# Cross-attention scores: probabilities as half-precision bits copied as 32-bit words, one maximum over two banks, and the exponential's table loaded at the stage's start

## The reference

```python
def _L0_xattn_ref(x, cond, Wq, bq, Wkv, bkv, Wp, bp):
    q = (x @ Wq + bq).reshape(1, B * N, H, hd)
    kv = (cond @ Wkv + bkv).reshape(1, -1, 2, H, hd)
    k, v = (kv[:, :, 0], kv[:, :, 1])
    ...
    q = _fq_sym(q, axis=-1)        # whole numbers from -127 to 127, times a step
    k = _fq_sym(k, axis=-1)
    v = _fq_sym(v, axis=2)
    attn = jnp.einsum('bhqd,bhkd->bhqk', q, k)
    attn = jax.nn.softmax(attn.astype(jnp.float32), axis=-1)
    attn = _fq_unsigned(attn, axis=-1)   # whole numbers from 0 to 255, times a step
    out = jnp.einsum('bhqk,bhkd->bhqd', attn, v)
    out = jnp.transpose(out, (0, 2, 1, 3)).reshape(B, N, C)
    return out @ Wp + bp
```

## Time and profile before

| | us |
|---|---|
| three runs | 1235.86, 1240.04, 1241.66 |
| median | 1240.04 |
| profiled execution | 1237.78 |
| its span, first to last instruction | 1236.1 |
| of that the scores stage (about 399 to 872) | 473 |
| PE, DVE, ACT busy over the span | 1003.9, 852.8, 700.4 |

### The profile page before, as it was taken

One profiled execution on the slowest core, in us unless ns is written; L12 is line 12 of the kernel. 1 busy time (PEld: TensorE's weight loads), 2 busy tenths in 40 slices (PEclk: granted clock), 3 DMA queues, 4 the chain that ended last, 5 costly groups with the idle time before them and its releaser, 6 DMA issues. The chain is left out here.

```text
span 1236.1 us, 21867 instructions
## 1 busy us (share of the span) xinstructions
PE 1003.9 (81%) x8049; PEld 682.7 (55%) x8049; DVE 852.8 (69%) x1409; ACT 700.4 (57%) x1039; POOL 243.6 (20%) x216
## 2 busy tenths in 40 slices
PE   4888996999457777777777777777779989999998
PEld 3745744888345444444444444444557765556566
DVE  6857546999687899999999999999661521111126
ACT  3453362455426899999999999999223202212221
POOL 1134063556250200000000000000533610000014
PEclk9999998999678799999999999999779989999999
DMA  8200004110000000000000000000040395131215
GB/s 320 96 1 1 1 2 154 51 34 17 9 0 13 31 1 2 1 0 0 0 0 0 0 0 0 0 0 0 1 151 27 135 379 230 60 116 64 69 56 182
DMA packets 24854, 68.14 MB, mean 55 GB/s; under 512 B 2722, under 2 KB 6818, under 8 KB 23778
## 3 DMA queue, kind: packets, MB, share of 16 engines
q1 hardware_dynamic: 20114, 52.48, 11.3%
q0 software_dynamic: 4400, 14.42, 3.7%
q10 hardware_dynamic: 288, 0.52, 0.1%
HBM read 49.07 MB, written 18.35 MB: 55 GB/s over the span
## 5 line engine op out<-in xcount | busy, mean ns | idle before, releaser
L1313 DVE TENSOR_REDUCE cs_top<-cs_s_b 128x1 f32<-128x512 f32 x256 | 164.8, 685 | 16.7 <-PE cs_s_b L1342 7.6
L1350 PE MATMUL cs_tp<-ident,cs_p_int 128*128 128x128 f16 x2048 | 158.4, 221 | 7.5 <-ACT cs_pT L1293 2.8
L1287 ACT ACTIVATE cs_p_int<-cs_s_b,cs_bias,cs_step_now 128x1024 int16<-128x1024 f32 x128 | 154.1, 1204 | 11.6 <-DVE cs_bias L1320 5.3
L1301 DVE TENSOR_REDUCE cs_top<-cs_s_a 128x1 f32<-128x1024 f32 x128 | 155.5, 1215 | 7.2 <-PE cs_s_a L1342 7.2
L1350 PEld LDWEIGHTS cs_tp<-ident,cs_p_int 128*128 128x128 f16 x2048 | 122.1, 98 | 60.3 <-issue 45.6
L1342 PE MATMUL cs_s_b<-k_parts,q_int 96*128 96x512 bf16 x256 | 79.0, 391 | 93.4 <-ACT cs_p_int L1287 93.1
L1287 ACT ACTIVATE cs_p_int<-cs_s_a,cs_bias,cs_step_now 128x1024 int16<-128x1024 f32 x128 | 152.8, 1194 | 0.0
L1293 ACT CAST cs_pT<-cs_tp 128x1024 bf16<-128x1024 int16 x128 | 129.5, 1012 | 3.3 <-PE cs_tp L1350 2.7
L2159 PE MATMUL ff_h<-ff_experts,ff_zgT 128*128 x368 | 115.1, 467 | 1.0 <-ACT ff_zgT L1798 0.9
L1446 POOL TENSOR_TENSOR co_o<-co_o,v_step 128x512 f32<-128x512 f32 x8 | 10.7, 1331 | 467.6 <-DVE co_o L1468 467.6
L1342 PE MATMUL cs_s_a<-k_parts,q_int 96*128 96x512 bf16 x256 | 79.4, 393 | 22.9 <-ACT cs_p_int L1287 18.7
(11 more groups left out here) (278 smaller groups left out, 2099.0 us busy)
## 6 DMA issues: line engine op xcount, KB each, us to landing
ff_experts<-in_experts_dram SPq DMA_DIRECT2D x8, 2176.0 KB, 14.6
slots<-sa_zero SPq DMA_DIRECT2D x1, 5888.0 KB, 25.8
ff_zg<-slots POOLq DMA_DIRECT2D x23, 256.0 KB, 2.9
run_y<-ff_yv SPq DMA_DIRECT2D x23, 256.0 KB, 2.0
ff_raw<-in_weights_dram SPq DMA_DIRECT2D x6, 768.0 KB, 5.8
ck_raw<-in_ctxT_dram SPq DMA_DIRECT2D x8, 512.0 KB, 3.3
stage<-in_cwkv_dram SPq DMA_DIRECT2D x2, 1024.0 KB, 6.8
out_dram<-x_res SPq DMA_DIRECT2D x8, 256.0 KB, 2.0
```

Source lines behind the costliest of these rows:

```text
L1287: nc.scalar.activation(p_int[:, u, half * HALF:(half + 1) * HALF], s[:, :], ACT.Exp, bias=bias[:, u:u + 1], scale=step_now[:, h:h + 1], ac ...
L1301: nc.vector.tensor_reduce(top[:, u, 0:1], s_a[u][:, :], AX_X, ALU.max).then_inc(max_ok, 1)
L1313: nc.vector.tensor_reduce(top[:, u, 1 + c:2 + c], s_b[:, c * 512:(c + 1) * 512], AX_X, ALU.max).then_inc(max_ok, 1)
L1350: ins = nc.tensor.transpose(tp[:, k, :], p_int[:, u, key:key + P].bitcast(F16), ident16[:, :])
```

## The change

- The copies out of `tp` no longer convert. `pT` becomes a 16-bit integer tile that holds the same bits as `p_int`, and the product reads it as half-precision floats, in which a whole number p up to 255 is p times 2^-24. ACT moves two of them at once as a 32-bit integer (at most 255 * 65536 + 255, less than 2^24); DVE's copy stays one of 16-bit elements. `v_int` becomes half precision. The output is multiplied by `P_UNIT` = 2^24 where it was copied (L1332).
- The two maxima over the banks of `s_b` become one over both, and `sb_ok` counts once per unit, after the second matmul.
- ACT computes a one-column exponential at the stage's start, ahead of its first unit.

```diff
+P_UNIT = 2.0 ** 24
...
-        pT = sb("cs_pT", [P, 2, KT, P], BF16)
-        top = sb("cs_top", [P, 2, 3], F32)
+        pT = sb("cs_pT", [P, 2, KT, P], I16)
+        top = sb("cs_top", [P, 2, 2], F32)
...
+        table = sb("cs_table", [P, 1], F32)
...
-                nc.scalar.copy(pT[:, u, HKT:KT, :], tp[:, :, :].bitcast(I16)).then_inc(rb_ok, 1)
+                nc.scalar.copy(pT[:, u, HKT:KT, :].rearrange("p k q -> p (k q)").bitcast(I32),
+                               tp[:, :, :].rearrange("p k q -> p (k q)").bitcast(I32)).then_inc(rb_ok, 1)
+            nc.scalar.activation(table[:, :], ident16[:, 0:1], ACT.Exp)
             units(act, step)
...
-                    for c in range(2):
-                        v_.wait_ge(sb_ok, 2 * n + c + 1)
-                        nc.vector.tensor_reduce(top[:, u, 1 + c:2 + c], s_b[:, c * 512:(c + 1) * 512], AX_X,
-                                                ALU.max).then_inc(max_ok, 1)
-                    v_.wait_ge(max_ok, 3 * n + 3)
+                    v_.wait_ge(sb_ok, n + 1)
+                    nc.vector.tensor_reduce(top[:, u, 1:2], s_b[:, :], AX_X, ALU.max).then_inc(max_ok, 1)
+                    v_.wait_ge(max_ok, 2 * n + 2)
...
-                    nc.vector.tensor_copy(o_raw[:, t - 1, :], out[:, :]).then_inc(out_read, 1)
+                    nc.vector.tensor_scalar(o_raw[:, t - 1, :], out[:, :], P_UNIT, None, ALU.mult).then_inc(out_read, 1)
...
-            def scores(t, h, s, half, made, each_bank=False):
+            def scores(t, h, s, half, made):
...
-                    if each_bank or c == 1:
-                        ins.then_inc(made, 1)
+                ins.then_inc(made, 1)
...
-                    scores(t, h, s_b, 1, sb_ok, each_bank=True)
+                    scores(t, h, s_b, 1, sb_ok)
...
-                        ins = nc.tensor.matmul(out[:, head * D:(head + 1) * D], pT[:, u, k, :],
+                        ins = nc.tensor.matmul(out[:, head * D:(head + 1) * D], pT[:, u, k, :].bitcast(F16),
...
-        v_int = sb("v_int", [P, KT, C], BF16)
+        v_int = sb("v_int", [P, KT, C], F16)
```

## The result

| | before | after |
|---|---|---|
| median of the runs made beside each other, us | 1236.58 (six, 1233.26 to 1241.66) | 1247.96 (six, 1246.95 to 1251.32) |
| profiled execution, us | 1237.78 | 1248.07 |
| its span, us | 1236.1 | 1246.3 |

The ratio is 1.009, with a 95% interval of 1.0063 to 1.0116: the changed kernel is slower by 11.4 us. The forecast was 11.6 us more than before. Its 1251.6 stood on the first three runs of before (median 1240.04); with three more that median is 1236.58, and this is nearly all of the 3.6 us between 1251.6 and 1247.96.

The account below looks back on a forecast made before the run. A closed loop ACT, PE, DVE, ACT around the single buffer `s_b` was taken as the bound, 3.54 us a period. Terms +16.7 - 0.5 - 2.8 - 0.4 - 1.4 = +11.6 us on median 1240.04 gave 1251.6 us, range 1243 to 1260.

Parts of the forecast that it names:

- The maximum's wait and merge: Usual `s_b` periods: waiting for both banks loses 0.22 us, merging wins 0.065; net 0.155 over 108 periods, +16.7 us.
- Units with the output's copy: Seven periods with DVE's finished-output copy: the wait costs nothing there and 0.065 us each is won, -0.5 us.
- Tile ends: Seven periods at a tile's end: ACT's shorter copy lets the loop's 3.695 us replace 4.09, -2.8 us.
- Table load and first bias: Stage's start: table load hidden in ACT's idle time and first bias 0.065 us earlier, -1.4 us.
- The last copy: After the last unit, PE waits for ACT's copy, which takes 0.425 us less: -0.4 us.
- The low-clock periods: Five periods at a granted clock near its lower level, bound by ACT or late transposes: taken as zero.
- DVE's work as the bound: Rival: DVE's work, not the loop, paces the stage, making the merge a gain; 1228 us, chance 0.06.
- A dearer 16-bit copy on DVE: Rival: DVE's copy out of `tp` takes 0.535 us more, 0.145 over its cover; +15.7, 1267 us, chance 0.03.
- a 32-bit copy on ACT that is no faster: Rival: ACT's integer copy gains nothing, so the -2.8 and -0.4 us fall away; 1255 us, chance 0.03.
- A second bank that comes sooner than modelled: Rival: waiting for the second `s_b` bank costs 0.10 us instead of 0.22; +0.8, 1241 us, chance 0.08.
- The pause of PE ahead of the `s_b` scores: Clock rival: this pause grows and the clock falls more often, at all seven tile changes; +3.5, 1255 us, chance 0.08.

Follow-up runs that it names:

- e1_two_maxima: The changed kernel with the two maxima per bank of `s_b` put back, each with its own wait; 1230.39 us, ratio 0.9934 to the kernel before.
- e2_merge_only: The kernel before with only the merged maximum over both `s_b` banks and one wait; 1253.81 us, ratio 1.0128 to before.
- e3_both_wait: The changed kernel with two maxima per bank of `s_b` again, both starting only after the second matmul; 1257.61 us, ratio 1.0166 to before.
- e6_extra_dve_after: The changed kernel with one extra, unread 128x384 DVE copy in every unit, behind the maximum over `s_a`; 1255.63 us, ratio 1.0164 to before.
- e5_per_bank_a: e4_split_exp with the maximum over `s_a` also taken per bank, each with its own wait; 1224.53 us, ratio 0.9913 to the kernel before.
- e4_split_exp: e1_two_maxima with the exponential of `s_b` split by bank, so PE refills the first while ACT reads the second; 1232.18 us, ratio 0.9957 to before.
- e7_extra_dve_two: e1_two_maxima with one extra, unread 128x384 DVE copy in every unit; 1249.2 us, ratio 1.0118 to the kernel before.

## Why the prediction was right

Point by point, from the profiled executions:

- *The maximum's wait and merge, 0.155 a period, +16.7 us.* Measured 0.15: lag 0.43 to 0.64, maximum to joining 1.32 to 1.26. At 108 periods that is 16.2. e1_two_maxima and e2_merge_only put all of the loss on it, e3_both_wait both of its halves.
- *Units with the output's copy, -0.065 each.* 3.96 became 3.89. Right.
- *Tile ends, 4.09 to 3.695, -2.8 us.* The release was named rightly, from ACT's copies to the bias, but the end is 3.84: -1.75 us. This term was the one most off. Two short delays that the sum left out show now: the exponential starts 0.33 behind the bias (579.95 to 580.28) where 0.25 is usual, and the maximum 0.71 behind the scores there (577.79 to 578.50), 0.07 over usual.
- *Table load and first bias, -1.4 us.* From the first maximum to the first exponential it was 4.45 (400.11 to 404.56) and is 3.10 (397.70 to 400.80): -1.35.
- *The last copy, -0.4 us.* From the last exponential of `s_b` to the copy of the last output it was 5.98 and is 5.55: -0.43.
- *The low-clock periods, zero.* Before there were five, two of them after the fall at 646 us; in the profiled execution after, the granted clock stayed at 1.00 from 640 to 656, and only the start was slow. That is about -0.7, in single executions.

First to last exponential of `s_b`: 460.6 to 473.6, +13.1 where the terms said +13.4; with start and tail +11.3 against +11.6. The rest of the two profiled executions differs by 1 us in the opposite direction: the stage began 2.4 us earlier, and what follows its last copy took 1.3 us longer, both in code that is the same. That 11.6 came within 0.2 of the 11.4 measured is luck in part. The gain at the tile ends was put 1.05 too high, the loss in the usual periods 0.5 too high, and the low-clock periods gave back 0.7 where nothing was expected: these errors cancel, and the 95% interval of the ratio spans some 8 to 14 us.

The rivals: DVE's work as the bound fell by e1, e2 and e6. A dearer 16-bit copy on DVE and a 32-bit copy on ACT that is no faster fell by two rows: DVE's copy is 0.68 as before, ACT's 0.58. A second bank that comes sooner than modelled, for 0.10 of wait, fell by the lag: it grew by 0.21. The pause of PE ahead of the `s_b` scores grew from 0.65 to 0.97 without a fall of the clock. The rule of the Trainium skill to minimize the number of operations ("VectorE: DVE Perf Modes", rules for kernel authors) holds for the engine's own time, 0.07 us a unit in e3_both_wait against the changed kernel. For the kernel's time it decided the wrong way, and e5_per_bank_a, with the most instructions, is the fastest.

What stays open: why the clock falls within the stage in some executions and places and not in others. It fell once in the profiled execution before, not once after, and at least once in each experiment's; in e6_extra_dve_after the raised periods follow a unit with the output's copy, in e2_merge_only and e3_both_wait (4.00 and 4.12, 4.19 and 4.18) a tile's end (granted clock 0.83 from 527 to 537 and 0.66 from 578 to 588 us). PE's pause alone does not tell them apart: behind each of the seven units with the output's copy it is 1.06 before, with one fall, and 1.17 after, with none. I made no run that changes the pause alone.

## What to carry to other kernels

Where a buffer is single, follow one round of the loop through every engine and add up starts to starts: if the sum is the period, the only edits that pay are those on that round, and a merge that must wait for the later of two producers costs the distance between the producers against the fixed cost of one instruction (0.22 against 0.07 us here). Two engines over 90% busy were not the bound. Before opening such a loop, measure the next one as well, over as many units as it has buffers; e4_split_exp won nothing until the second was opened too.

## What was not expected of the hardware

The extra DVE copy in e6_extra_dve_after, SBUF to SBUF, takes 0.35 us. Once it took ten times that, beside an operation of GpSimd with two inputs in SBUF:

```profile
402.32 0.35 DVE L1327 COPY cs_extra<-v_int 128x384 f32<-128x384 f32 x1
...
405.19 4.50 POOL L1266 TENSOR_TENSOR wp_lo<-stage,wp_hi 128x2048 fp32r<-128x2048 f32 x1
...
406.64 3.27 DVE L1327 COPY cs_extra<-v_int 128x384 f32<-128x384 f32 x1
```

It ended at 409.91, 0.22 after GpSimd's end at 409.69. The DVE instruction just before, a maximum over PSUM from 405.50 for 1.23 us, ran at its usual length beside the same GpSimd operation. The Trainium skill ("GPSIMD Engine Reference", the table of specifications) says that GpSimd shares its SBUF interfaces with VectorE, with contention where VectorE runs in a mode that uses two ports or has two SBUF inputs; these rows agree, but none of them shows in which mode the copy ran. The period with it took 6.69 us instead of 3.69. The same happened in e7_extra_dve_two: a copy of 2.93 us, again ending 0.22 after GpSimd's operation, in a period of 6.71.
